# Queries, keys and transposed inputs in half-group shares inside the attention steps, norms on GpSimd

## What is computed

```python
def attention(q, latent_kv, Wq, Wkv, Wout):        # 16 heads of 32
    qp, (k, v) = q @ Wq.T, split(latent_kv @ Wkv.T)
    scores = einsum('bhqd,bhkd->bhqk', qh, kh) * 32 ** -0.5
    attn = softmax(where(causal, scores, lowest))
    return (attn @ vh) @ Wout.T

x = x + attention(layernorm(x), ctx, Wq, Wkv, Wout)
h = layernorm(x)
p, i = top_k(softmax(h @ gate.T), 2)               # 8 experts
x = x + sum(p * expert_i(h)) + sigmoid(h @ g.T) * shared(h)
```

## Time and profile before

| | |
|---|---|
| median of 3 executions | 1713.71 us (1713.55 to 1717.65) |
| the profiled execution | 1713.32 us |
| its span, first to last instruction | 1711.5 us |
| mean granted TensorE clock | 0.972 |
| busy over the span: TensorE | 1586.7 us (93%) |
| VectorE, ScalarE, GpSimd | 883.5 (52%), 616.5 (36%), 463.2 us (27%) |

### The profile page before, as it was taken

How to read it: one execution, slowest core, us unless ns; L and a number is a source line. 1 busy time by engine, 2 the same in 40 slices (tenths; PEclk the granted TensorE clock), 3 DMA queues, 4 the chain that set the end, 5 groups by cost and what they waited for, 6 DMA issues and landing times.

```text
span 1711.5 us, 30372 instructions
## 1 busy us (share of the span) xinstructions
PE 1586.7 (93%) x10524; PEld 1329.2 (78%) x10524; DVE 883.5 (52%) x1724; ACT 616.5 (36%) x1945; POOL 463.2 (27%) x424
## 2 busy tenths in 40 slices
PE   4899899889993599999999999999999999999998
PEld 4677767767772499999999997888888888888886
DVE  4556675676565467676667675442232323232322
ACT  4766676576670232333332333321111111111111
POOL 3111312313213455655555550201000000000010
PEclk9899999999995699999999999999999999999999
DMA  5122322322122466666666664413020203021110
GB/s 186 52 61 86 87 83 59 86 80 75 43 87 44 152 236 238 259 243 240 240 232 249 244 254 161 140 70 111 13 99 25 98 25 98 25 86 36 50 49 25
DMA packets 82445, 202.43 MB, mean 118 GB/s; under 512 B 37424, under 2 KB 38448, under 8 KB 77648
## 3 DMA queue, kind: packets, MB, share of 16 engines
q1 hardware_dynamic: 70208, 168.44, 28.6%
q0 software_dynamic: 12176, 33.20, 5.9%
HBM read 153.64 MB, written 47.97 MB: 118 GB/s over the span
## 4 chain that ended last, share of the span: by engine, by line
PE 79%; DVE 8%; ACT 5%; issue 3%; DMA 1%; POOL 1%; another core or an unknown queue 1%; DVEq 0%; SPq 0%; ACTq 0%; POOLq 0%
PE psum L542 51%; PE psum L776 12%; PE psum L726 9%; ACT probs L849 2%; PE psum L699 2%; ACT probsT L834 2%; DVE smax L1159 2%; DVE stat L1093 1%; PE psum L596 1%; DVE v_sb L1166 1%; PE psum L587 1%; PE psum L605 1%; POOL lists_dram L1010 1%; PE psum L660 1%
## 5 line engine op out<-in xcount | busy, mean ns | idle before, releaser
L542 PE MATMUL psum<-nT_hi,ws_hi 128*128 128x512 f32 x616 | 243.1, 395 | 3.5 <-DVE nT_lo L1374 3.5
L542 PE MATMUL psum<-nT_hi,ws_lo 128*128 128x512 f32 x616 | 244.9, 398 | 0.0
L542 PE MATMUL psum<-nT_lo,ws_hi 128*128 128x512 f32 x616 | 244.4, 397 | 0.0
L1413 DVE TENSOR_TENSOR h_s<-psum,silu_s 128x512 f32<-128x512 f32 x77 | 53.2, 692 | 364.8 <-PE psum L542 360.5
L542 PE MATMUL psum<-gT_hi,wj_hi 128*128 128x256 f32 (+1 forms) x840 | 233.9, 278 | 1.2 <-DVE gT_lo L1345 1.2
L542 PE MATMUL psum<-gT_lo,wj_hi 128*128 128x256 f32 (+1 forms) x840 | 233.4, 278 | 0.0
L542 PE MATMUL psum<-gT_hi,wj_lo 128*128 128x256 f32 (+1 forms) x840 | 233.3, 278 | 0.0
L1072 POOL DMA_INDIRECT routed<-expert_out_dram,slot_b x56 | 55.2, 986 | 575.4 <-DVE slot_b L1426 383.2
L849 ACT ACTIVATE probs<-psum,minus_max 112x112 f32<-112x112 f32 x512 | 175.2, 412 | 16.5 <-DVE minus_max L1161 16.4
L1034 POOL TENSOR_SCALAR wj_hi<-wj_raw 128x2816 fp32r<-128x2816 f32 x68 | 136.8, 2028 | 145.1 <-PE psum L726 118.4
L1364 DVE TENSOR_TENSOR wj_lo<-wj_raw,wj_hi 128x2816 fp32r<-128x2816 f32 x70 | 170.3, 2434 | 5.7 <-issue 3.3
(11 more groups left out here) (193 smaller groups left out, 3108.4 us busy)
## 6 DMA issues: line engine op xcount, KB each, us to landing
wj_raw<-in_w_experts SPq DMA_DIRECT2D x35, 2176.0 KB, 8.6
expert_out_dram<-y_c SPq DMA_DIRECT2D x35, 512.0 KB, 2.7
wj_raw<-in_w_shared SPq DMA_DIRECT2D x11, 768.0 KB, 4.4
x_in<-in_x SPq DMA_DIRECT2D x32, 224.0 KB, 3.5
x_res<-in_x SPq DMA_DIRECT2D x32, 224.0 KB, 3.0
x_dram<-x SPq DMA_DIRECT2D x32, 224.0 KB, 2.3
normed_dram<-xn SPq DMA_DIRECT2D x32, 224.0 KB, 3.1
normedT_dram<-xn2T SPq DMA_DIRECT2D x32, 224.0 KB, 3.5
```

Source lines behind the costliest of these rows:

```text
L542: mm = pe.matmul(out_ap, u, v, start=(n == 0), stop=(n == last))
L1413: dve.tensor_tensor(h_s[:, :], bank(b), silu_s[:, :], ALU.mult).then_inc(emptied_b[b], 1)
```

## The change

The front as a stage of its own is gone. Only the first half group is made ahead (`first_front`). After that every step ends with `next_front`: the queries and the keys of two of the four channel blocks for half a group (`HT` = 224 columns, 24 and 6 products), the half of two steps later, and the transposes of one batch of four steps later. So steps 0 and 1 of a group make its own second half, steps 2 and 3 the first half of the next one. An evacuation now covers two blocks of 224 columns, or the four blocks of one batch. The table gives the queries bank 5, the keys bank 7 and the transposed inputs bank 6.

Both norms (`xn1`, `xn2`) move from VectorE to GpSimd, each right behind its inverse root; `xn2` is made in the step that makes its statistics. The context is split by half groups. The eight scatters of a group are delayed to the next round and go out three, three and two in its first three steps. On VectorE the first choice and the places stand behind the row maxima; the lo part of one batch's `xT` stands ahead of them. On ScalarE the router's exponentials go behind `aT_hi`. Wq is loaded before the third and fourth input, and on ScalarE and VectorE its split and Wout's stand between shares of the first front. Four groups are written out in place of three.

```diff
-PEELED = 3
+PEELED = 4
 GT = TB * SEQ
+HT = GT // 2
...
-         (("xT", 0, 5), ("xT", 1, 4), ("k", 0, 6), ("k", 1, 7), ("xT", 2, 5), ("xT", 3, 4), ("k", 2, 6), ("k", 3, 7),
-          ("q", 0, 5), ("q", 1, 4), ("q", 2, 6), ("q", 3, 7))]
+         (("x0", 0, 5), ("x0", 1, 4), ("k0", 0, 6), ("k0", 1, 7), ("q0", 0, 5), ("q0", 1, 4), ("x0", 2, 6), ("x0", 3, 7))]
...
+    TURNS += [((_j, "q", 0), -2, 5), ((_j, "k", 0), -2, 7), ((_j, "xT", 0), -TB, 6)]
...
+        def half_of(j):
+            return (HT, GT) if j < 2 else (0, HT)
+        def halves_split(g, j):
+            return 2 * g + (2 if j < 2 else 3)
...
-            def front(g):
...
+            def queries(b, ms, at, to):
+                for i, m in enumerate(ms):
+                    cols = slice(m * P, (m + 1) * P)
+                    mm = product(psum[:, b, i * HT:(i + 1) * HT], [((wq_hi[:, k, cols], wq_lo[:, k, cols]), (xT_hi[:, k, at:to], xT_lo[:, k, at:to]))
+                                                                   for k in range(KC)])
...
+            def next_front(g, j):
+                at, to = half_of(j)
+                if there(g, j, -2):
+                    if j == 0 and is_first(g):
+                        for i in (2, 3):
+                            wait_emptied(pe, 0, -1, "x0", i)
+                    elif j % 2 == 0:
+                        wait_emptied(pe, g, j - 1, "xT")
+                    queries(take(g, j, "q"), HALVES[j % 2], at, to)
+                    pe.wait_ge(S["ctx_split"], halves_split(g, j))
+                    keys(take(g, j, "k"), HALVES[j % 2], at, to)
+                if there(g, j, -TB):
+                    pe.wait_ge(S["xn1_ready"], g * TB + j + TB + 1)
+                    rows_across(take(g, j, "xT"), j)
...
-                    if j == 0:
-                        for m in range(KC):
-                            wait_emptied(pe, g, -1, "q", m)
                     for m in range(KC):
+                        if j % 2 == 0 and m % 2 == 0:
+                            front_ready(pe, g, j, "q", m)
+                            front_ready(pe, g, j, "k", m)
...
+                next_front(g, j)
             def body(g):
-                if there(g, -1, 0):
-                    front(g)
+                if is_first(g):
+                    first_front()
...
+            def first_front():
+                for j in range(2):
+                    x_hi(0, -1, "x0", j, turns.bank("x0", j))
+                weights_hi(0)
+                for i in range(2):
+                    evacuate(0, -1, "k0", i, kT, HALVES[i], 0, HT)
+                weights_hi(1)
+                for i in range(2):
+                    evacuate(0, -1, "q0", i, qT, HALVES[i], 0, HT)
+                for j in range(2, 4):
+                    x_hi(0, -1, "x0", j, turns.bank("x0", j))
+                weights_hi(2)
...
+                    if there(g, j, -2):
+                        evacuate(g, j, "q", 0, qT, HALVES[j % 2], *half_of(j))
+                        evacuate(g, j, "k", 0, kT, HALVES[j % 2], *half_of(j))
+                    if there(g, j, -TB):
+                        x_hi(g, j, "xT", 0, turns.bank("xT"))
...
+            def norm1(j, n):
+                inverse_root(mv1, rs1, j % 2, "stats1", "rstd1_made", n)
+                pool.wait_ge(S["rstd1_made"], 2 * n)
+                settled(pool)
+                pool.tensor_scalar(xn1[:, j, :], x_in[:, j, :], mv1[:, j % 2, 0:1], rs1[:, j % 2, 1:2],
+                                   ALU.subtract, ALU.mult).then_inc(S["xn1_ready"], 1)
...
             def body(g):
                 for j in range(TB):
                     t = g * TB + j
+                    if j == 0 and before(g, NG):
+                        split_context(2 * g + 2, g, 1)
+                    if j == 2 and before(g, NG - 1):
+                        split_context(2 * g + 3, g + 1, 0)
                     if before(g, NG - 1):
-                        inverse_root(mv1, rs1, j % 2, "stats1", "rstd1_made", t + TB + 1)
-                    if j == TB - 1 and before(g, NG - 1):
-                        split_context(g + 1)
+                        if is_first(g):
+                            wait_filled(pool, 0, -1, "x0", j)
+                        else:
+                            wait_filled(pool, g - 1, j, "xT")
+                        norm1(j, t + TB + 1)
+                    if routes(g - 1) and before(g, NG + 1):
+                        if j == 0:
+                            if isinstance(g, int) and g == 3:
+                                pool.wait_ge(S["lists_zeroed"], 16)
+                            else:
+                                move_ids(g - 3)
+                        if j < 3:
+                            scatter(g - 2, ITEMS[3 * j:3 * j + 3])
                     if there(g, j, 2):
                         inverse_root(mv2, rs2, j % 2, "stats2", "rstd2_made", t - 1)
-                if routes(g):
...
+                        if there(g, j, 4):
+                            wait_filled(pool, g, j - 1, "normT")
+                            pool.wait_ge(xn2_stored[j % 2], 16 * (2 * g + j // 2 - 1))
+                        pool.wait_ge(S["rstd2_made"], 2 * (t - 1))
                         settled(pool)
+                        pool.tensor_scalar(xn2[:, j % 2, :], x1[:, j % 2, :], mv2[:, j % 2, 0:1], rs2[:, j % 2, 1:2],
+                                           ALU.subtract, ALU.mult).then_inc(S["xn2_ready"], 1)
+                if isinstance(g, int) and g >= NG:
+                    if g == NG:
+                        move_ids(g - 2)
+                    scatter(g - 1, ITEMS)
...
             stats1(0, 1, 1)
             stats1(1, 2, 1)
-            norm1(0, 1)
+            for n in range(2):
+                x_lo(0, -1, "x0", n, n)
+            weights_lo(0)
             stats1(2, 3, 1)
-            norm1(1, 2)
             stats1(3, 4, 1)
-            norm1(2, 3)
-            norm1(3, 4)
-            for n in range(3):
-                weights_lo(n)
+            weights_lo(1)
+            for n in range(2, 4):
+                x_lo(0, -1, "x0", n, n)
+            weights_lo(2)
...
-                if there(g, j, 3):
-                    dve.wait_ge(S["rstd2_made"], 2 * (t - 2))
-                    if there(g, j, 5):
-                        dve.wait_ge(xn2_stored[(j + 1) % 2], 16 * (2 * g + (j - 3) // 2))
-                    normalise(xn2[:, (j + 1) % 2, :], x1[:, (j + 1) % 2, :], mv2, rs2, (j + 1) % 2).then_inc(S["xn2_ready"], 1)
-                if j == 0 and routes(g):
-                    choose(g - 1, 0)
-                if j == TB - 1 and routes(g):
-                    place(g - 1)
+                if there(g, j, 1 - TB) and not (is_first(g) and j == 0):
+                    x_lo(g, j - 1, "xT", 0, t + TB - 1)
                 if there(g, j, 0):
                     dve.wait_ge(S["scores_done"], t + 1)
...
                         dve.tensor_reduce(smax[:, 2 * i:2 * i + 2, :], scores, AX.X, ALU.max).then_inc(S["smax_made"], 1)
                         dve.wait_ge(S["smax_made"], 2 * t + i + 1)
                         dve.tensor_scalar(minus_max[:, 2 * i:2 * i + 2, :], smax[:, 2 * i:2 * i + 2, :], -SCALE, None, ALU.mult).then_inc(S["max_made"], 1)
+                if j == 0 and routes(g):
+                    choose(g - 1, 0)
+                if j == TB - 1 and routes(g):
+                    place(g - 1)
...
-                if before(g, NG - 1):
-                    if j == 0:
-                        wait_filled(dve, g, -1, "xT", 3)
-                    norm1(j, t + TB + 1)
```

171 lines of the change are left out of this document (86 added, 85 removed).

## The result

The changed kernel took 1703.18 us in the median (1701.64 to 1704.32, five runs), the kernel before 1713.71 (1712.53 to 1717.65) beside it: a ratio of 0.9938, 95% interval 0.9922 to 0.9954. So it is faster by 10.5 us, beyond the 5 us that can be told, but by less than half of the 24.1 us that I forecast, and inside my range (1668 to 1710). The profiled execution has a span of 1701.1 us against 1711.5.

The account below looks back on a forecast made before the run. Only the attention loop is touched, its steps tight on TensorE and ScalarE at once. The terms -1.5 - 9.7 - 0.95 - 17.9 + 6.9 - 1 = -24.1 us take 1713.7 to 1689 us; range 1668 to 1710.

Parts of the forecast that it names:

- The mechanism of the front: Attention steps: query and key products move into each step; TensorE alone sets 14.2 us, ScalarE having 4 us of slack.
- (e): Last attention group, 44.55 us before: now makes its own second half in its first two steps, +6.9 us.
- (f): Behind the attention loop: the drained chain stays, but one group's scatters go out in portions, -1 us, at most -3.
- a step over 15 us: Sign that the forecast is wrong: an attention step this long, with the engine named before the masks or the projection.
- The price of a narrow product: Query and key products over 224 columns on TensorE: 0.105 us each, ends 0.100 and 0.117, thirty making 3.15 a step.
- (c): Second attention group, the last without routing, 57.75 us before: -0.95 us.
- (d): Five routing groups of the attention loop, 61.78 us each before and 58.2 forecast: 5 x -3.6 = -17.9 us.
- My account of the 4.0 us: Routing groups' excess over 57.75 us before: waits for the value copy 0.65 and 1.95, lower TensorE level 1.4.
- The start: Up to the second group: -1.5 us until the first row maxima (from -8 to +4), then -9.7 in the first group.
- the norms covered: Both norms on GpSimd, 0.6 to 1.3 us each, are made over 4 us before TensorE needs them: no cost.
- Waits stay: Rival, chance 0.14: TensorE's waits move but remain, one more us in each of 24 steps; 1700 to 1714 us.
- GpSimd becomes the bound: Rival, chance 0.04: norms stretched beside VectorE's work need up to 18 us in steps with scatters; 1749 us.

## Why the prediction was wrong, point by point

**Right.** The mechanism of the front: it goes into the steps, TensorE alone sets them, ScalarE waits for the query evacuation (2.2 to 3.3 us), no step waits for exponentials once the first group is over, and the dip of TensorE behind the fourth step's wait is gone. (e) and (f) hold within 0.5 us. The choice ahead of the value copy costs 0.8 us, where I said 0.9. (With it a first step is 15.2 us, which my sign "a step over 15 us" counts as wrong although my own sum had 15.1.)

**The price of a narrow product** was the term on which everything hung. I took 0.105 from the meeting of stream and load, between ends of 0.100 and 0.117, and 0.1114 it is, plus 0.08 for the first of a run. The step at fault is the floor: I scaled 0.101 from the router's products over nine columns, which are plain fp32 and have 112 weight columns, and no row of before had the floor of this type. The columns alone (0.100) would have allowed the price; the floor of 0.1114 did not. 0.28 us by 24 steps are 6.7 us, and (c) and (d) together missed by 6.5. Spreading the front therefore gains nothing as such: four steps of 14.48 are 57.9 us, where 57.75 stood. All of the routing groups' gain comes from waits that the longer step can hide. My account of the 4.0 us that these waits and the dip cost before was also too neat, though the sum did not use it: it left out the rank products, and it put the dip of 1.4 us into every group, where only three of the five had it (granted clock 0.97; the two at 1.00 took 61.06 and 60.47 us).

**The start** missed by 4.6 us, 3.0 of it ahead of the first row maxima (+1.5 in place of -1.5) and 1.6 behind them. I had the right pieces (Wq's split behind the key evacuations, Wout's ahead of the maxima) and sized them too small: "about 2" was 4.76 us of wait plus some 2 us at TensorE's lower level, "another 2.5" was 3.7. And I called the norms covered "more than 4 us before TensorE asks for them", and gave them 0.6 to 1.3 us. They take 2.08, and at the start, where two of them stand in a row ahead of the first transposes, nothing covers them.

**Phases C and B** I left out of the sum, as the change does not touch them. They took 3.4 us more in this pair of profiles, about 2 by the medians of all; why, no run shows.

**The rivals.** None came in as written. "Waits stay" had the time (1700 to 1714) but not the cause: the steps had their slack. That the time fell into my range is owed to the room that I had left for rivals which did not come. "GpSimd becomes the bound" named VectorE's work as what would stretch it, which happened once, at the start (4.22 us beside Wq's split). What the experiments met was the reverse and elsewhere: GpSimd's scatters, issued beside large transfers, made VectorE and ScalarE late. The first profile of the changed kernel has none of this, so it explains nothing of the miss. The trace of before had it already, as query evacuations 4.1 to 4.7 us late, and I passed over them because nothing waited for them there.

## What to carry to other kernels

When products are made narrower, ask for the price of one that is as narrow, of the same type and with as many weight columns; if no row has it, take the floor from none of another type. Halving the columns doubles the count, and here it stopped paying below 256 columns. Work of another engine fits behind a step's critical operation only if the step has room: with the places between maxima and value copy, the projection waited 2.71 us in a step of 10.7 us and 0.40 in one of 14.4. Moving work off an engine also moves what stands behind it in its queue: look where those instructions land, indirect DMAs above all, and put them by a wait where no large transfer runs; it cost nothing here, and on one chip it gave 26.7 us.
